# Addresses of the matmul operands modulo 512 bytes, and the order of two opening steps, in a cross-attention block on one core

## What is computed

```python
tgt1 = _layer_norm(tgt, g1, be1)
tgt = tgt + _self_attn(tgt1, mask, Wq, bq, Wk, bk, Wv, bv, Wo, bo)
tgt = tgt + (memory @ Wg.T + bg)
tgt1 = _layer_norm(tgt, g2, be2)
ff = jax.nn.relu(tgt1 @ W1.T + b1) @ W2.T + b2
return tgt + ff
```

## Time and profile before

| | |
|---|---|
| median of three runs | 1826.27 us (1825.44 to 1827.51) |
| the profiled execution | 1827.06 us |
| its span in the profile | 1825.4 us |
| TensorE busy | 1783.9 us (98%) |
| ScalarE busy | 1465.5 us (80%) |
| VectorE busy | 1351.8 us (74%) |
| GpSimd busy | 869.5 us (48%) |
| mean granted TensorE clock | 0.99 of full |

### The profile page before, as it was taken

How to read it: one execution, slowest core, us unless ns; L and a number is a source line. 1 busy time by engine, 2 the same in 40 slices (tenths; PEclk the granted TensorE clock), 3 DMA queues, 4 the chain that set the end, 5 groups by cost and what they waited for, 6 DMA issues and landing times.

```text
span 1825.4 us, 53743 instructions
## 1 busy us (share of the span) xinstructions
PE 1783.9 (98%) x17972; PEld 1756.9 (96%) x17972; DVE 1351.8 (74%) x6810; ACT 1465.5 (80%) x5577; POOL 869.5 (48%) x907
## 2 busy tenths in 40 slices
PE   6799999999999999999999999999999999999997
PEld 5699999999999999999999999999999999999997
DVE  6677777777777777777777777777777777777762
ACT  4788888888887887887887887887887887887882
POOL 2254454454454454444444444444444444444454
PEclk7899999999999999999999999999999999999999
DMA  6665665665765765755755755755755755755730
GB/s 163 94 97 97 113 96 97 114 95 97 116 94 97 117 93 97 118 92 95 121 90 94 122 90 95 122 88 97 123 87 98 122 87 99 121 87 99 112 70 18
DMA packets 148931, 183.66 MB, mean 101 GB/s; under 512 B 14768, under 2 KB 99120, under 8 KB 148656
## 3 DMA queue, kind: packets, MB, share of 16 engines
q1 hardware_dynamic: 148656, 180.23, 59.3%
HBM read 62.73 MB, written 16.78 MB: 44 GB/s over the span
## 4 chain that ended last, share of the span: by engine, by line
PE 95%; ACT 1%; issue 0%; DMA 0%; DVE 0%; SPq 0%; ACTq 0%
PE ffn_ps L793 14%; PE ffn_ps L795 13%; PE ffn_ps L794 13%; PE turn_ps L858 12%; PE work_ps L793 9%; PE work_ps L795 8%; PE work_ps L794 8%; PE score_ps L844 7%; PE value_ps L884 6%; PE work_ps L810 3%; PE turn_ps L868 2%; ACT scores L366 1%; DMA k_stack<-k_hi 0%; ACT hid L409 0%; SPq L317 0%
## 5 line engine op out<-in xcount | busy, mean ns | idle before, releaser
L366 ACT ACTIVATE scores<-scores,row_min 128x128 f32<-128x128 f32 x2048 | 795.6, 400 | 2.6 <-DVE row_min L599 1.7
L719 POOL TENSOR_TENSOR hT_lo<-hid,hT_hi 128x512 fp32r<-128x512 f32 x256 | 356.5, 1392 | 575.2 <-DVE hT_hi L629 575.2
L376 ACT ACTIVATE probs<-turn_ps 128x512 f32<-128x512 f32 x512 | 302.8, 592 | 241.0 <-PE turn_ps L858 241.0
L599 DVE CUSTOM_DVE_ANT_0 scores<-score_ps,mask_bias 128x128 f32<-128x128 f32 x2048 | 470.9, 286 | 1.8 <-issue 1.8
L366 ACT ACTIVATION_READ_ACCUMULATOR scores<-scores,row_min 128x1 f32 x2048 | 406.6, 199 | 0.0
L858 PE MATMUL turn_ps<-ident,scores 128*128 128x128 f32 x2048 | 308.3, 273 | 3.3 <-ACT probs L376 3.2
L793 PE MATMUL ffn_ps<-zT_hi,w_lo 128*128 128x256 f32 x1024 | 305.1, 298 | 5.0 <-ACT hid L409 4.2
L793 PE MATMUL ffn_ps<-w_hi,hT_lo 128*128 128x256 f32 x1024 | 304.6, 297 | 2.4 <-ACT hid L409 2.4
L795 PE MATMUL ffn_ps<-w_hi,hT_hi 128*128 128x256 f32 x1024 | 289.2, 282 | 0.0
L795 PE MATMUL ffn_ps<-zT_hi,w_hi 128*128 128x256 f32 x1024 | 289.1, 282 | 0.0
L794 PE MATMUL ffn_ps<-zT_lo,w_hi 128*128 128x256 f32 x1024 | 288.8, 282 | 0.0
(11 more groups left out here) (113 smaller groups left out, 4279.7 us busy)
## 6 DMA issues: line engine op xcount, KB each, us to landing
q_stack<-q_hi SPq DMA_DIRECT2D x128, 256.0 KB, 6.9
k_stack<-k_hi SPq DMA_DIRECT2D x256, 128.0 KB, 6.4
x_in<-x_dram SPq DMA_DIRECT2D x64, 256.0 KB, 2.8
mem_in<-memory_dram SPq DMA_DIRECT2D x64, 256.0 KB, 6.9
x_res<-x_dram SPq DMA_DIRECT2D x64, 256.0 KB, 6.9
q_stack<-q_lo SPq DMA_DIRECT2D x64, 256.0 KB, 4.2
k_stack<-k_lo SPq DMA_DIRECT2D x128, 128.0 KB, 6.2
out_dram<-y SPq DMA_DIRECT2D x64, 256.0 KB, 2.1
```

The costliest lines, as they stand in the source:

```text
L366: last = act.activation(exps, exps, ACT.Exp, bias=row_min[:, k, h:h + 1], scale=-1.0, accum_out=row_sum[:, k, h:h + 1])
L376: act.activation(probs[:, k, :], turn_ps[k % 2][:, :], ACT.Copy).then_inc(probs_copied, 1)
L599: last = dve.tensor_tensor_reduce(out=scores[:, slot(i, t), h, :], in0=score_ps[t % 2][:, h * S:(h + 1) * S], in1=mask_bias[:, b, :], scal ...
L719: pool.tensor_tensor(halves[1], src, halves[0], ALU.subtract).then_inc(done, 1)
```

## The change

The tensors are placed in another order, so that their addresses modulo 512 differ. By the sizes, they come out as follows:

| address modulo 512 | tensors |
|---|---|
| 0 | wq, wk |
| 320 | zT, k_stack |
| 384 | q_stack, wv, wo, wg, w1, w2, and ident, scores, probs, v_pad and all others up to y |
| 448 | xT, attnT, memT, hT |

In each of the 172 matmuls of 256 columns the streamed operand then lies 64 bytes below the loaded one, modulo 512 (xT at 448 under wq at 512, for one). The transposes and the value matmuls keep operands with equal addresses modulo 512.

In the order of the work, VectorE takes the statistics of `x_in` behind the low part of k in tick 5, in every iteration. The low parts of o, g and 2 are made by GpSimd ahead of `set_zeros(1)`, and VectorE keeps that of 1; ScalarE makes the high parts in the order o, g, 2, 1. A semaphore `split_more` counts GpSimd's three, and ScalarE waits for it before it first overwrites `probs` (which held the raw w2), TensorE before the first projection and the first hidden product.

```diff
+        weight("q", KT * D)
+        weight("k", KT * D)
+        row_min, row_sum = sb("row_min", [P, CHUNKS, CH]), sb("row_sum", [P, CHUNKS, CH])
+        one = sb("one", [P, H])
+        zT = [sb("zT_hi", [P, KT, ROWS], F32R), sb("zT_lo", [P, KT, ROWS], F32R)]
+        k_stack = [sb(f"k_stack{n}", [P, CPB, 2, KT * GB, S], F32R) for n in range(2)]
+        stats1 = sb("stats1", [P, GB, 6])
+        q_stack = [sb(f"q_stack{n}", [P, CPB, KT, ROWS], F32R) for n in range(2)]
+        for n in "vog":
+            weight(n, KT * D)
+        weight("1", KT * FF)
+        weight("2", FT * D)
...
+        stats2 = sb("stats2", [P, GB, 6])
+        xT = [sb("xT_hi", [P, KT, ROWS], F32R), sb("xT_lo", [P, KT, ROWS], F32R)]
+        attnT = [sb("attnT_hi", [P, KT, ROWS], F32R), sb("attnT_lo", [P, KT, ROWS], F32R)]
+        memT = [sb("memT_hi", [P, KT, ROWS], F32R), sb("memT_lo", [P, KT, ROWS], F32R)]
         hT = [sb("hT_hi", [P, FT, ROWS], F32R), sb("hT_lo", [P, FT, ROWS], F32R)]
...
+                if k == 0 and not later(g):
+                    act.wait_ge(split_more, MORE_AT["2"])
...
-                for n, name in enumerate("og12"):
+                for name in "og21":
                     act.wait_ge(weight_loaded[name], 16)
...
-                for n, name in enumerate("og12"):
-                    dve.wait_ge(weights_hi, n + 1)
-                    low_part(name)
+                dve.wait_ge(weights_hi, 4)
+                low_part("1")
...
-                            dve.wait_ge(split_lo, SPLIT_AT["2"])
+                            dve.wait_ge(split_lo, SPLIT_AT["1"])
...
-                    if norm and t == 5:
-                        dve.wait_ge(x_loaded, 16 * (i + 3))
-                        layer_norm_stats(i + 2, x_in, stats1, mv1, ln1_rstd, ln1_stats, ln1_mean)
...
                         last.then_inc(k_split, 1)
+                    if norm and t == 5:
+                        dve.wait_ge(x_loaded, 16 * (i + 3))
+                        layer_norm_stats(i + 2, x_in, stats1, mv1, ln1_rstd, ln1_stats, ln1_mean)
...
-            def second_zeros():
+            def low_parts_and_zeros():
                 pool.wait_ge(ln1_rstd, 2)
+                for n, name in enumerate("og2"):
+                    pool.wait_ge(weights_hi, n + 1)
+                    pool.tensor_tensor(weights[name][1][:], raw(name), weights[name][0][:], ALU.subtract
+                                       ).then_inc(split_more, 1)
+                pool.wait_ge(split_more, 3)
                 pool.wait_ge(scores_ready, 1)
                 set_zeros(1)
...
-                    pe.wait_ge(split_lo, SPLIT_AT["2"])
+                    pe.wait_ge(split_lo, SPLIT_AT["1"])
+                    pe.wait_ge(split_more, MORE_AT["2"])
...
-                            pe.wait_ge(split_lo, SPLIT_AT["g"])
+                            pe.wait_ge(split_more, MORE_AT["g"])
```

More of the change, by code:

```diff
@@ L102, in sem, with weight @@
             return ctx.enter_context(nc.semaphore(name))
[L105 to L110, removed]
         weights = {}
-        for n, cols in (("q", KT * D), ("k", KT * D), ("v", KT * D), ("o", KT * D), ("g", KT * D),
-                        ("1", KT * FF), ("2", FT * D)):
+        def weight(n, cols):
             weights[n] = (sb(f"w{n}_hi", [P, cols], F32R), sb(f"w{n}_lo", [P, cols], F32R))
+        weight("q", KT * D)
[10 more added lines that the diff above has]
+        weight("2", FT * D)
         def tiles(n, k):
@@ L120, in xattn_block @@
         w1, w2 = tiles("1", KT), tiles("2", FT)
+        ident = sb("ident", [P, P])
+        row = sb("row", [P, 4, D])
+        bvw, bow, bgw, b2w = (row[:, n, :] for n in range(4))
         x_in = sb("x_in", [P, GB, D])
         xhat = sb("xhat", [P, GB, D])
-        xT = [sb("xT_hi", [P, KT, ROWS], F32R), sb("xT_lo", [P, KT, ROWS], F32R)]
         q = [sb("q_hi", [P, KT, ROWS], F32R), sb("q_lo", [P, KT, ROWS], F32R)]
         kk = [sb("k_hi", [P, KT, ROWS], F32R), sb("k_lo", [P, KT, ROWS], F32R)]
-        q_stack = [sb(f"q_stack{n}", [P, CPB, KT, ROWS], F32R) for n in range(2)]
-        k_stack = [sb(f"k_stack{n}", [P, CPB, 2, KT * GB, S], F32R) for n in range(2)]
         v_pad = [sb(f"v_pad{n}", [P, GB, H, 2 * HD]) for n in range(2)]
@@ L141, in xattn_block @@
         attn = sb("attn", [P, KT, ROWS])
-        attnT = [sb("attnT_hi", [P, KT, ROWS], F32R), sb("attnT_lo", [P, KT, ROWS], F32R)]
         mem_in = sb("mem_in", [P, KT, ROWS])
-        memT = [sb("memT_hi", [P, KT, ROWS], F32R), sb("memT_lo", [P, KT, ROWS], F32R)]
         x_res = sb("x_res", [P, GB, D])
@@ L147, in xattn_block @@
         xhat2 = sb("xhat2", [P, GB, D])
-        zT = [sb("zT_hi", [P, KT, ROWS], F32R), sb("zT_lo", [P, KT, ROWS], F32R)]
         resid_b2 = sb("resid_b2", [P, GB, D])
         hid = sb("hid", [P, 2, 2, ROWS])
+        y = sb("y", [P, GB, D])
+        stats2 = sb("stats2", [P, GB, 6])
+        xT = [sb("xT_hi", [P, KT, ROWS], F32R), sb("xT_lo", [P, KT, ROWS], F32R)]
+        attnT = [sb("attnT_hi", [P, KT, ROWS], F32R), sb("attnT_lo", [P, KT, ROWS], F32R)]
+        memT = [sb("memT_hi", [P, KT, ROWS], F32R), sb("memT_lo", [P, KT, ROWS], F32R)]
         hT = [sb("hT_hi", [P, FT, ROWS], F32R), sb("hT_lo", [P, FT, ROWS], F32R)]
-        y = sb("y", [P, GB, D])
         vector_cols, at = {}, 0
@@ L162, in xattn_block @@
         bqc, bkc = qk_bias[:, 0:KT], qk_bias[:, KT:2 * KT]
-        stats1, mv1 = sb("stats1", [P, GB, 6]), sb("mv1", [P, GB, 2])
+        sum_inv = sb("sum_inv", [P, GB, KT, CPB, 2])
+        mv1, mv2 = sb("mv1", [P, GB, 2]), sb("mv2", [P, GB, 2])
         var1, var2 = sb("var1", [P, GB]), sb("var2", [P, GB])
         carrier = sb("carrier", [P, CHUNKS])
-        stats2, mv2 = sb("stats2", [P, GB, 6]), sb("mv2", [P, GB, 2])
         rstd1, rstd2 = sb("rstd1", [P, GB]), sb("rstd2", [P, GB])
-        one = sb("one", [P, H])
         eps, minus_half = sb("eps", [P, GB]), sb("minus_half", [P, GB])
@@ L185, in xattn_block @@
         split_hi, weights_hi, split_lo = sem("split_hi"), sem("weights_hi"), sem("split_lo")
+        split_more = sem("split_more")
         rows_summed, constants_set = sem("rows_summed"), sem("constants_set")
@@ L243, in xattn_block @@
                  "1": (w1T, KT), "2": (w2T, FT)}
-        SPLIT_AT = {n: j + 1 for j, n in enumerate(SETUP)}
+        SPLIT_AT = {n: j + 1 for j, n in enumerate("qkv1")}
+        MORE_AT = {n: j + 1 for j, n in enumerate("og2")}
         SHIFTED = "qkv1"
@@ L761, in iteration @@
                                            ALU.add).then_inc(resid_biased, 1)
-            run(pool, iteration, after_second=second_zeros)
+            run(pool, iteration, after_second=low_parts_and_zeros)
         @block.tensor
```

## The result

The changed kernel takes 1807.12 us (median of four runs, 1806.92 to 1808.42), the kernel before 1826.17 us beside it. The ratio is 0.9896, its 95% interval 0.9879 to 0.9914. That is 19 us less where 40 were forecast: the direction and the range held, the size did not. The profiled execution took 1808.42 us, 18.64 less than that of before.

The account below looks back on a forecast made before the run. TensorE's matmul step bounds the kernel, a ring of scores, q and copies close behind. From 1827.06 us, 36 for steady groups, 2 behind them and 2.3 for the opening leave 1786.8 profiled, forecast 1786 us; range 1766 to 1826.

Parts of the forecast that it names:

- the ring: Each group's loop: scores to q issue 11.96 us, stack transfers 14.67, landing wait 0.24; binds at 26.87, gaining 0.59 us.
- TensorE binds before: Steady groups of the kernel before: TensorE sets the 27.46 us period; the copies' loop has 0.79 or 0.40 us slack.
- The step falls with the distance of 64 bytes: 172 matmuls of 256 columns a group: start-to-start step from 120 to 112 ns, 1.38 us a group for TensorE alone.
- the rule that spoke against this part: Skill's rule of two independent read ports: addresses would not matter, and the sum would lose its 38 us.
- Any step below about 116 ns ends here.: Steady groups: below about 116 ns a matmul, the copies' loop holds the period at 26.87 us.
- soft-ring rival: Steady groups: step 109 ns, landing wait 0.1 us, copies' loop 26.64 us; 1770 us in all, chance 0.20.
- Behind the last group, 2 us: After the steady stretch: some 350 more matmuls at 8 ns give 2.8 us, of which 2 us are taken.
- The opening, 2.3 us: Before the steady stretch: low parts moved off VectorE let xT_lo start 2.2 us earlier; 2.3 us gained, bounds 0.6 and 3.5.
- GpSimd adds three subtractions: Opening: GpSimd's low parts of o, g and w2 take 8.4 us, fit ahead of its zeroing and cost nothing.
- moves by no more than the hole: Opening: k_lo moves earlier, but the k transfers' landing only by the gap in busy DMA engines, put at 0.6 us.
- Half a cure: Rival: step falls only to 118 ns, TensorE still bounds, 24 us gained, 1802 us; chance 0.18.
- The slower rival: Rival: at 64 bytes all 172 matmuls a group settle at a 125 ns step, 1878 us; chance 0.10.

Follow-up runs that it names:

- before_short: The kernel before, with the second copy of the high parts left out of the stack transfers and as many matmuls; 1822.26 us, period 27.46 us.
- after_short: The changed kernel, with the second copy of the high parts left out of the stack transfers and as many matmuls; 1783.88 us, period 26.85 us.
- offm64: The changed kernel with streamed operands 64 bytes above the loaded ones instead of 64 below; 1815.01 us.
- off128: The changed kernel with streamed operands 128 bytes below the loaded ones instead of 64; 1817.07 us, ratio 0.9946 to the kernel before.
- off256: The changed kernel with streamed operands 256 bytes away from the loaded ones; 1829.00 us.
- loads_late: The changed kernel, but SyncE issues the loads of mem_in and x_res only after the k transfers land; 1789.84 us, ratio 0.9801 to the kernel before.

## Why the prediction fell short

The mechanism held, TensorE's step and then the ring. What failed is the sum for the ring, 26.87 us a group against 27.17, and the 2.3 us for the opening.

**TensorE binds before.** Right, shown by before_short: 3.4 us less of copies changed no period.

**The step falls with the distance of 64 bytes.** Right in direction. I took 112 ns from between the transposes' 109 and 115; it is 115.4, so the estimate for a duration that is 5 ns shorter was the better one. By my sum this size did no harm: it is still under the 116 ns from which the ring was to take over. What I took from the rule that spoke against this part, that addresses would not matter, fell. By the Trainium skill, "TensorE: Matmul & The Clock Gate", section "Step-by-step: what each phase is for", a load doesn't steal read bandwidth from the running matmul; five distances with steps from 115.4 to 119.6 ns show that the addresses matter all the same, by a way that stays open.

**The ring takes over, "12.20 - 0.24 = 11.96, plus the transfers' mean of 14.67, plus the wait", 26.87 us.** The mechanism is right (46 of 56 groups wait for the landing) and the sum failed: 12.18 + 14.88 + 0.11 = 27.17. Three terms were mis-sized.
- The copies: +0.21 against my 14.67, +0.26 against before's mean. "They add no instruction" was taken to mean that the addresses change nothing for the DMA engines. The runs show 0.26 us for `k_stack` at 320. This term is a cost of the change itself that I never priced, and the same addresses that help TensorE bring it.
- The leg from the scores to the q issue: 0.02 us shorter and not 0.24. In it ScalarE is busy 9.84 of the 10.13 us from xT_hi to the q issue (the window 603.37 to 613.50 above). SyncE waits for q_lo, which VectorE makes behind hT_hi, and hT_hi waits for ScalarE's `hid`; the lines stand below this list. A leg on ScalarE's path doesn't shrink because matmuls beside it do. I wrote that the rest is ScalarE's and VectorE's work and still counted 30 matmuls in series with it. This is read from the trace; no run shortened ScalarE's part.
- The wait between landing and scores: 0.11 and not 0.24, which gave 0.13 back.

```profile
611.60 0.43 DVE L635 CAST hT_hi<-hid 128x512 fp32r<-128x512 f32 x1 [1.33 <-ACT hid L419]
...
612.55 0.87 DVE L648 SCALAR_TENSOR_TENSOR q_lo<-work_ps,qk_bias,q_hi 128x256 fp32r<-128x256 f32 x2
```

0.21 + 0.22 - 0.13 = 0.30 us a group, times 61 = 18 us of the 21 that were missing.

**"Any step below about 116 ns ends here."** With my 26.87 us for the ring this came out only by luck. TensorE's own period is 26.85 us at 115.5 ns (after_short), just under it. The real ring, 27.17 us, takes over from a longer step on: at 117.6 ns (offm64) the scores of 34 of 56 groups still start within 0.12 us of the landing, at 118.6 (off128) those of 5. Removing the ring alone would not have given the soft-ring rival's 1770 us at this step: after_short takes 1783.88.

**Behind the last group, 2 us.** It was 1.6.

**The opening, 2.3 us.** Wrong, -0.4. xT_lo of the second group began 0.55 us earlier (36.99 after 37.54) and not 2.2. The step that failed is "GpSimd adds three subtractions", which was put down as costing nothing: I looked for GpSimd's idle time and not for what VectorE runs meanwhile, and xhat waits 2.8 us. The bound of 0.6 us, "if a new wait takes the rest", named the right kind of thing with too small a price. `x_in`'s later landing took 0.9 us more, and the leg with the longer stretch at the lower clock level 1.0 us; I had priced neither. That the landing of the k transfers "moves by no more than the hole" held as a bound: k_lo came 4.25 us earlier. The 0.6 us that I took from it didn't come; the first scores start at 33.7 us as against 33.3.

**The rivals.** "Half a cure" gave 1802 us and is nearest to the time, but for a wrong reason: its step was 118 ns and TensorE bound. The run had a better step and a binding ring. The slower rival, a worse step from the new distance, did not come; no distance that was tried has a longer step than none.

## What to carry to other kernels

When an engine at 98% gets faster, price the next chain term by term from its own rows, and ask of each term which engine's work it is: only a leg on the engine that got faster shrinks. An edit that only moves addresses touches everyone who reads or writes there, the DMA engines too, so list the transfers whose ends move. And the cure for a ring of copies may be a transfer that isn't in it: here one wait, which holds back two loads that could come later without harm, brought 17 us.

## What the runs showed of the hardware

- In a stream of matmuls of 256 columns with a load beside each, the mean start-to-start step depends on the streamed operands' addresses against the loaded ones', modulo 512 bytes: 119.6 ns at equal addresses, 115.4 with all streamed ones 64 bytes below, 117.6 with them 64 above, 118.6 at 128 below, 119.5 at 256. Giving the 16 score matmuls of a group alone the good distance didn't shorten their step (121.0 after 120.0 ns).
- How long a DMA copy within the chip's memory takes depends on its destination's address: nine transfers of 1.5 MB in all take 14.62 us with both stacks at 384 modulo 512, 14.88 with one at 320, 15.14 with both. The rule behind it stays open. The Trainium skill, "DMA: Bandwidth & Descriptors", section "How a descriptor splits into AXI transactions", lets a start off a 256-byte boundary cost extra, and speaks there of bytes that are fetched. It doesn't explain what the destinations cost: off256, with both stacks on such a boundary, had the slow 14.93 us, and 384, which is off it, the fast 14.62 (residues counted as above).
- A VectorE instruction that meets a running GpSimd one can wait for all of it: 0.73 us became 3.53 behind a subtraction, and 5.26 while GpSimd zeroed memory. Not every one does: v_pad, which reads `work_ps`, kept its 0.89 us beside the same subtraction.
- Loads issued behind a row of copies still slow the copies down: held back until the landing, they leave copies of 14.53 us instead of 14.88 (loads_late).
